# Last column transposes in another PSUM bank, six turn buffers, an earlier first tile of half two, and another order around the passage to layer 1

## The reference

```python
h = maximum(layernorm(x), 0)
# layer 0
S = relu((adj + adj.T) * 0.5); D = sum(S, axis=1); d = where(D > 0, D ** -0.5, 0)
L = eye - d[:, None] * S * d[None, :]
x = x + relu(L @ (h @ W0))
# layer 1
h = maximum(layernorm(x), 0)
x = x + diag(adj) @ (h @ W1[0]) + triu(adj, 1) @ (h @ W1[1]) + tril(adj, -1) @ (h @ W1[2]) + bias
```

## Time and profile before

| | |
|---|---|
| median of 3 runs | 958.63 us (954.3, 958.63, 959.94) |
| profiled execution, its own time | 957.01 us |
| its span in the profile | 955.2 us |
| PE busy | 909.1 us (95%) |
| DVE, ACT, POOL busy | 554.8, 492.6, 292.5 us |
| share of PE in the chain that ended last | 88% |
| mean granted TensorE clock | 0.992 |

### The profile page before, as it was taken

One profiled execution on the slowest core, in us unless ns is written; L12 is line 12 of the kernel. 1 busy time (PEld: TensorE's weight loads), 2 busy tenths in 40 slices (PEclk: granted clock), 3 DMA queues, 4 the chain that ended last, 5 costly groups with the idle time before them and its releaser, 6 DMA issues.

```text
span 955.2 us, 17248 instructions
## 1 busy us (share of the span) xinstructions
PE 909.1 (95%) x4471; PEld 767.5 (80%) x4471; DVE 554.8 (58%) x1461; ACT 492.6 (52%) x1042; POOL 292.5 (31%) x300
## 2 busy tenths in 40 slices
PE   3578999999999999999999998999999999999998
PEld 2467788888888888888888887888888888888886
DVE  3896777777878875656565655443433343334432
ACT  2898557666676665455545554343333333333331
POOL 4785344344434444434443441111111100000000
PEclk9999999999999999999999999999999999999999
DMA  9995799999999985565556556666666655555552
GB/s 285 312 273 149 251 317 333 321 352 322 349 323 339 340 286 207 176 198 161 158 177 196 165 163 192 199 202 189 192 183 185 192 167 164 167 164 159 162 169 68
DMA packets 179577, 212.68 MB, mean 223 GB/s; under 512 B 13648, under 2 KB 114000, under 8 KB 177488
## 3 DMA queue, kind: packets, MB, share of 16 engines
q1 hardware_dynamic: 136816, 158.18, 54.8%
q10 hardware_dynamic: 42720, 54.01, 16.2%
HBM read 143.99 MB, written 68.16 MB: 222 GB/s over the span
## 4 chain that ended last, share of the span: by engine, by line
PE 88%; DVE 3%; ACT 3%; DMA 2%; SPq 2%; issue 1%; ACTq 0%; DVEq 0%
PE psAcc L570 23%; PE psAcc L568 23%; PE psAcc L569 23%; PE psA L436 3%; PE psG L539 2%; PE psG L541 2%; PE psG L540 2%; PE psZ L501 2%; PE psW L408 1%; DMA colb<-in_adj 1%; ACT hst L600 1%; PE psG L408 1%; SPq L248 1%; PE psAcc L582 1%; PE psAcc L581 1%
## 5 line engine op out<-in xcount | busy, mean ns | idle before, releaser
L636 ACT ACTIVATE Lh<-C 128x512 fp32r<-128x512 f32 x256 | 161.5, 631 | 291.7 <-PE psAcc L570 249.4
L568 PE MATMUL psAcc<-Xh,Lh 128*128 128x512 f32 x496 | 199.7, 403 | 1.8 <-issue 1.4
L568 PE MATMUL psAcc<-Yh,Lh 128*128 128x512 f32 x512 | 200.9, 392 | 0.0
L570 PE MATMUL psAcc<-Yh,Ll 128*128 128x512 f32 x512 | 200.1, 391 | 0.0
L569 PE MATMUL psAcc<-Yl,Lh 128*128 128x512 f32 x512 | 199.9, 390 | 0.0
L570 PE MATMUL psAcc<-Xh,Ll 128*128 128x512 f32 x496 | 194.4, 392 | 0.0
L569 PE MATMUL psAcc<-Xl,Lh 128*128 128x512 f32 x496 | 194.0, 391 | 0.0
L823 DVE TENSOR_TENSOR Ll<-C,Lh 128x512 fp32r<-128x512 f32 x128 | 91.0, 713 | 142.9 <-ACT Lh L636 142.8
L570 PEld LDWEIGHTS psAcc<-Yh,Ll 128*128 128x128 f32 x512 | 96.1, 188 | 20.1
L569 PEld LDWEIGHTS psAcc<-Yl,Lh 128*128 128x128 f32 x512 | 96.2, 188 | 18.9
L568 PEld LDWEIGHTS psAcc<-Yh,Lh 128*128 128x128 f32 x512 | 96.2, 188 | 18.7
(11 more groups left out here) (130 smaller groups left out, 1356.5 us busy)
## 6 DMA issues: line engine op xcount, KB each, us to landing
C<-at_dram SPq DMA_DIRECT2D x128, 256.0 KB, 2.7
at_dram<-AT SPq DMA_DIRECT2D x16, 1088.0 KB, 5.4
s_dram<-C ACTq DMA_DIRECT2D x64, 256.0 KB, 5.4
R<-in_adj SPq DMA_DIRECT2D x64, 256.0 KB, 6.1
g_dram<-g ACTq DMA_DIRECT2D x32, 512.0 KB, 4.2
C<-s_dram SPq DMA_DIRECT2D x64, 256.0 KB, 3.9
C<-in_adj SPq DMA_DIRECT2D x60, 256.0 KB, 5.5
t_dram<-x ACTq DMA_DIRECT2D x32, 256.0 KB, 2.6
```

Source lines behind the costliest of these rows:

```text
L568: mm(acc, lh, rh[:, k, :], start=k == 0, stop=False)
L570: mm(acc, ll, rh[:, k, :], start=False, stop=c < L1 and k == NB - 1).then_inc(used, 1)
L636: A(Lh[:, q, :], C[:, q, :], ACT.Relu if s.c < L1 else ACT.Copy).then_inc(lhi, 1)
```

## The change

- The last group's column transposes go to `psW`, as all others do, and no longer wait for the turned tiles. `product0(12)` goes to `psAcc[:, 1]`, and `times_W0(13)`, which overwrites `psW`, waits for the reduction of all 7 groups.
- The turned tiles have six buffers instead of four (`x1[:, 1]` and `xe` are added).
- The prologue is written by tables only, slots -1 to 55. Within a slot ACT scales and splits before it normalises and turns; DVE does the degrees and rests before the statistics.
- The first xp: statistics on DVE in slot 39, ahead of the last `degrees`; the power on POOL behind the last `root`; normalised on ACT ahead of `scaled_hi(12)`; transposed ahead of the last two `rows_T` of step 0. In step 1 POOL's power for the second xp stands ahead of the masks, and ACT normalises it before it splits a quarter; its product with W0 stands after block 3 and not 7.
- Passage: SP loads the first `lx` and `g2` earlier in step 31; in steps 32 and 33 `slot` stands ahead of the last two `gev_out` and `t_out`; the first `result` is moved from the start of step 33 to its end on DVE.

```diff
-        SCALE_AT = [12, 13, 19, 20, 25, 26, 31, 32, 35, 36, 39]
+        COLS_AT = [9, 16, 22, 28, 32, 36, 40]
+        DEG_AT = [9, 17, 23, 29, 33, 37, 40]
+        ROOT_AT = [8, 16, 22, 28, 32, 36, 40]
+        TIMES_AT = [11, 12, 18, 19, 24, 25, 30, 31, 34, 35, 39, 40, 42, 42, 43, 43]
+        HIGH_AT = [12, 13, 19, 20, 25, 26, 31, 32, 35, 36, 39, 40, 44, 44, 44, 44]
+        LOW_AT = [14, 15, 21, 22, 27, 28, 33, 34, 37, 38, 40, 41, 44, 44, 44, 44]
+        MAIN_AT = [18, 19, 24, 25, 33, 34, 37, 38, 42, 42, 44, 44, 47, 47, 47, 47]
+        ROWS_AT = [41, 41, 46, 46]
+        COPY_AT = [42, 42]
+        XP_STAT, XP_POWER, XP_MEAN, XP_NORMAL, XP_TURN, SUM_AT = 39, 40, 42, 43, 45, 43
-        T0 = [z[:, :], h2[:, :], g12[:, 0, :], g12[:, 1, :]]
+        T0 = [z[:, :], h2[:, :], g12[:, 0, :], g12[:, 1, :], x1[:, 1, :], xe[:, :]]
-            return psZ[:, :] if j == 12 else psW[:, :] if j == 13 else psG[:, j % 2, :]
+            return psAcc[:, 1, :] if j == 12 else psW[:, :] if j == 13 else psG[:, j % 2, :]
@@ SP, body @@
+                    if q == 1 and c == L1 - 1:
+                        load_lx(nxt)
+                        load_g2(nxt)
-                if c == L1 - 1:
-                    load_lx(nxt)
-                    load_g2(nxt)
@@ PE, columns0 @@
-                dst = psW if e < len(GROUPS) - 1 else psAcc[:, 1, :]
-                if e == len(GROUPS) - 1:
-                    pe.wait_ge(t0_ok, NB)
@@ PE, times_W0 @@
                 if j == 13:
-                    pe.wait_ge(d_cols, len(GROUPS) - 1)
+                    pe.wait_ge(d_cols, len(GROUPS))
@@ ACT, turned0 @@
-                wait(act, w0_ok, j - 3)
+                wait(act, w0_ok, j - NT + 1)
@@ ACT, body @@
+                if L1 <= c < L1 + 2:
+                    slot(t)
                 if 2 <= c < L1 + 2:
                     gev_out(t, 2)
                     gev_out(t, 3)
-                if c >= L1:
+                if c >= L1 + 2:
                     slot(t)
@@ DVE, prologue @@
+                if XP_STAT == n:
+                    dve.wait_ge(ld_xp, 16)
+                    stats(npn, xp, p_st, p_mv, p_ve, 1)
+                if XP_MEAN == n:
+                    dve.wait_ge(p_rs, 1)
+                    neg_mean(npn, p_nm)
@@ DVE, body @@
-                if c > L1:
+                if c > L1 and c != L1 + 1:
                     result(t)
...
+                if L1 <= c < L1 + 2:
+                    slot(t)
                 if 2 <= c < L1 + 2:
                     t_out(t, 2)
                     t_out(t, 3)
                     wait(dve, tev, t.of(4, -4))
+                if c == L1 + 1:
+                    result(t)
                 if c < LAST - 1:
                     split_lo(nxt, 2)
-                if c >= L1:
+                if c >= L1 + 2:
                     slot(t)
```

More of the change, by code:

```diff
@@ L452, in _, with chunk_T @@
             pe.wait_ge(ld_w, 32)
-            for n, (k, g) in enumerate(CH0):
+            def chunk_T(n):
+                k, g = CH0[n]
                 i = NB - 1 - k
@@ L467, in _, with turn @@
                 last.then_inc(p0T, 1)
-                for e in range(len(COLS_AT)):
+            def turn(src, sem):
+                for b in range(HB):
+                    last = nc.tensor.transpose(psZ[:, b * F:(b + 1) * F], src[:, b * F:(b + 1) * F], ident[:, :])
+                last.then_inc(sem, 1)
+            for n in SLOTS:
+                if 0 <= n < len(CH0):
+                    chunk_T(n)
+                for e in range(len(GROUPS)):
                     if COLS_AT[e] == n:
@@ L473, in _ @@
                         turn0(j)
-                for j in range(len(SCALE_AT)):
-                    if SCALE_AT[j] - 1 == n:
+                for j in range(NB):
+                    if TIMES_AT[j] == n:
                         times_W0(j)
-                for j in range(len(MAIN_AT)):
+                for j in range(NB):
                     if MAIN_AT[j] == n:
                         main0(j)
[L480 to L502, removed]
+                for q in range(NQ):
+                    if ROWS_AT[q] == n:
+                        pe.wait_ge(p0S, len(CH0) - (1 if q % 2 == 0 else 0))
+                        rows_T(Step(None, 1), q)
+                if XP_TURN == n:
+                    pe.wait_ge(p_h, 1)
+                    pe.wait_ge(t0_ok, NB)
+                    turn(xp, yT)
             def finish(t, k):
                 c = t.c
-                if k == (7 if c == 1 else 3) and 1 <= c <= NB:
+                if k == 3 and 1 <= c <= NB:
                     if c == 1:
@@ L547, in body @@
                 if c == 1:
[L548 removed]
+                    pe.wait_ge(prep_lo, 13)
                 elif c < L1 + 2:
@@ L606, in turned0 @@
                 act.wait_ge(t0, j + 1)
-                wait(act, w0_ok, j - 3)
-                A(T0[j % 4], turned(j), ACT.Copy).then_inc(t0_ok, 1)
+                wait(act, w0_ok, j - NT + 1)
+                A(T0[j % NT], turned(j), ACT.Copy).then_inc(t0_ok, 1)
             def scaled_hi(j):
@@ L672, in turned_xp @@
                 A(yTs[:, :], psZ[:, :], ACT.Copy).then_inc(yT_ok, 1)
[L674 to L679, removed]
+            for n in SLOTS:
+                if 0 <= n < len(CH0):
+                    rectify(n)
+                for j in range(NB):
+                    if HIGH_AT[j] == n:
+                        scaled_hi(j)
+                for q in range(NQ):
+                    if SPLIT_HI_AT[q] == n:
+                        split_hi(Step(None, 0), q)
+                for j in range(NB + 1):
+                    if j < NB and NORMAL_AT[j] == n:
+                        normal0(j)
+                    if j and TURNED_AT[j - 1] == n:
+                        turned0(j - 1)
+                for q in range(2):
+                    if COPY_AT[q] == n:
+                        copy_T(Step(None, 1), q)
+                if XP_NORMAL == n:
+                    normal_xp(Step(None, 0))
             split_hi(Step(None, 1), 0)
-            normal_xp(Step(None, 0))
+            turned_xp(Step(None, 0))
             split_hi(Step(None, 1), 1)
             copy_T(Step(None, 1), 2)
-            turned_xp(Step(None, 0))
             split_hi(Step(None, 1), 2)
@@ L853, in degrees @@
                 w = min(hi, NB - 1) - lo
-                src = psW if e < len(GROUPS) - 1 else psAcc[:, 1, :]
                 dve.wait_ge(p0D, e + 1)
-                V.reduce_sum(drow[:, lo:lo + w, NQ], src[:, 0:w * P].rearrange("p (j c) -> p j c", c=P),
+                V.reduce_sum(drow[:, lo:lo + w, NQ], psW[:, 0:w * P].rearrange("p (j c) -> p j c", c=P),
                              axis=AX.X).then_inc(d_cols, 1)
@@ L883, in _ @@
                                 rowb[:, (NB - 1 - k) % 3, 4 * g * P:4 * g * P + w], ALU.add).then_inc(p0S, 1)
[L884 to L890, removed]
+            for n in SLOTS:
+                if 0 <= n < len(CH0):
+                    chunk_sum(n)
+                for e in range(len(GROUPS)):
                     if DEG_AT[e] == n:
                         degrees(e)
-                for j in range(len(SCALE_AT)):
-                    if SCALE_AT[j] + 2 == n:
+                for u in range(NB // 2):
+                    if MEAN_AT[u] == n:
+                        mean0(u)
+                for j in range(NB):
+                    if LOW_AT[j] == n:
                         scaled_lo(j)
-                for q in range(NQ - 1):
-                    if SPLIT_AT[q] + 2 == n:
+                for q in range(NQ):
+                    if SPLIT_LO_AT[q] == n:
                         split_lo(Step(None, 0), q)
[L899 to L911, removed]
+                if SUM_AT == n:
+                    sum_T(Step(None, 1), 0)
+                if XP_STAT == n:
[4 more added lines that the diff above has]
+                    neg_mean(npn, p_nm)
+                for j in range(NB):
+                    if STAT_AT[j] == n:
+                        stats0(j)
             split_lo(Step(None, 1), 0)
```

90 lines of the change are left out of this document (47 added, 43 removed).

## The result

The changed kernel takes **964.53 us** (median of 11 runs, 961.03 to 967.29); the kernel before took 958.63 in the same comparison (11 runs, 954.3 to 959.94). The ratio is 1.006, 95% interval 1.0045 to 1.0075: slower by 5.9 us, within 1% of no change. The profiled execution of the changed kernel took 967.29 us, span 965.4, the slowest of its 11.

A forecast was written before the change was run, and what follows sets the result against it. The prediction took PE to bound the steps. Its terms, -3.9 + 5.4 + 1.7 - 3.9 + 2.5 + 1.7 = +3.5 us, gave 960.5 on the profiled 957.01 or 962.1 on the median; it said 961 us, range 953 to 967.

The forecast's parts named there:

- two new waits: PE waits at the prologue's end (+5.4 us) and in step 34 (+2.5 us), each with +1.7 us of low clock.
- two gains: Second xp in step 1, -3.9 us, and the passage of steps 32 to 34, -3.9 us.
- First xp on DVE, +5.4 and +1.7: Prologue end: DVE waits for xp's load before the last degrees, holding PE's `times_W0(13)` 5.4 us; low clock adds 1.7.
- Column transposes, buffers, slot order, 0: Prologue: the 0.84 us wait before column transposes goes, but under the new wait; 0, or 0.8 without that wait.
- Second xp, -3.9: Step 1: an earlier load removes PE's wait before the second xp turn, 2.27 us, and the low clock, 1.66 us.
- `lx` -1.8, slots -1.5 and -0.6: Passage, steps 32 to 34: earlier `lx` load and slot copies remove PE's waits; together -3.9 us.
- `result` and the store, +2.5 and +1.7: Steps 33 and 34: the store waiting for late `result` delays SP's loads; PE waits 2.5 us, low clock adds 1.7.
- rival C: Both holds longer: later xp, work behind the reduction not fitting, or burst at 284 GB/s; 963 to 967 us, chance 0.16.
- rival A: Passage clean: burst at 408 GB/s or above, or loads overtake, so `t_dram` is in time; 956 to 958 us, chance 0.23.
- The clock behind a wait in a dense stretch: Step 34: a short wait may leave PE's clock alone, making the sum 1.7 us lower.
- The base: Whole kernel: +3.5 us on the profiled 957.01 gives 960.5; on the median 958.63 it gives 962.1; 961 was said.

The follow-up runs named there:

- the repeat: The changed kernel, unaltered, run once more for one profile: 965.52 us.
- Experiment 1: Changed kernel with SP issuing the first xp load ahead of the last strip's load: 958.56 us, ratio 0.9993 to the kernel before.
- experiment 11: Changed kernel with first xp load ahead of the last strip, step 33's store behind its loads, and four turn buffers instead of six: 954.08 us.
- experiment 5: Changed kernel with first xp load ahead of the last strip's load and step 33's store behind that step's loads: 954.06 us, ratio 0.9956 to the kernel before.
- experiment 10: Kernel before with only the changed passage and step 33's store behind that step's loads; prologue, steps 1 and 2 untouched: 955.53 us, ratio 0.9957.
- experiment 8: Changed kernel with the loads of lx and g2 for step 32 back at the end of SP's step 31: 966.65 us.
- experiment 9: Changed kernel with the two slot copies of steps 32 and 33 back behind the last evictions on ACT and DVE: 964.85 us.
- experiment 4: Changed kernel with SP issuing the store of step 33 behind that step's loads instead of ahead: 959.25 us, ratio 1.0006 to the kernel before.
- experiment 7: Changed kernel with first xp load and step 33's store moved, ACT's step 1 xp load issued earlier, early normalising extended to step 2: 955.43 us.

## Why the prediction was right, and where it was not

The forecast was 961 us in 953 to 967, by two new waits that outweigh two gains. 964.5 lies in the range, 3.5 above the forecast. That it is not further off is in part luck, since errors cancel: the first hold was forecast 1.1 us too high, the hold of step 34 by the medians 1.1 too low, and the gain on the second xp 2.4 too high. By its steps:

- **First xp on DVE, +5.4 and +1.7.** The mechanism was right, the size a little high. PE's `times_W0(13)` started 7.23 us later than in the trace before, 4.5 more than its prologue was; in the repeat 5.9 later, 5.1 more. From there to step 1 it lost 1.6 us to the low clock in both. Experiment 1 took 6.0 away, against the 7.1 of the forecast.
- **Column transposes, buffers, slot order, 0.** Right for the whole. The 0.8 us that I kept for a prologue without hold did not show: from the last chunk on ACT to `times_W0(13)` experiment 1 takes 4.7 us and the kernel before 4.8. In the trace of experiment 1 PE waits 1.60 us for ACT's z there, a wait that the trace before doesn't have at that place; that this took the place of the 0.84 us is my reading. The six buffers are worth 0 by experiment 11.
- **Second xp, -3.9.** The two parts were there, -3.8 in both traces of the changed kernel. What failed is that the prediction let PE keep all of it and put nothing against it in step 2. PE, no longer at 0.50, reached the turn of step 2 ahead of the chain on ACT and DVE and gave back 1.7 us in the repeat and 3.2 in the first trace (2.6 of it the wait, the rest stands under no wait). In the trace before that chain had its time from the low clock: experiment 5 enters step 2 2.78 us ahead of it, but ACT begins to normalise the xp of step 2 only 0.27 us ahead (127.76 against 128.03). The step fails as "the wait costs 2.27 and the low clock 1.66": removed, they are worth about 1.5, by experiment 5 against 10. This is the largest missed term, 2.4 us.
- **`lx` -1.8, slots -1.5 and -0.6.** Right: -3.7 by alignment, in both traces of the changed kernel and in experiments 5 and 10; of it the loads are 2.1 by the medians of experiment 8 and 1.8 by its alignment, and the slots 1.9 by the alignment of experiment 9.
- **`result` and the store, +2.5 and +1.7.** The mechanism was right, the size not: 5.9 us by the alignment, 5.3 by experiment 4, against 4.2. The burst did go out at 284 GB/s, the lowest of my three rates, and took 10.4 us; I had chosen between 284 and 334. That is rival C's rate and makes the forecast wait 3.5 us in place of 2.5. The rest lies in a row that I read wrongly. I took 0.68 us for the split of quarter 3 of step 34, the length of most splits, but this one took 1.62 us in the trace before already, and 1.59 in the changed kernel:
```profile
610.52 1.62 DVE L823 TENSOR_TENSOR Ll<-C,Lh 128x512 fp32r<-128x512 f32 x1
```
  With it the forecast wait would have been 4.4 us. Why it is longer than the others is open. The wait was 4.02 + 0.16 = 4.2 us and the low clock behind it 1.7. In the repeat the wait was 4.1 and the low clock cost 2.6; there the granted clock was 0.50 from 617 us on, 1.6 us before PE resumed. By the Trainium skill, page DMA: Bandwidth & Descriptors, section Where 436 GB/s comes from, the ceiling of the ports is 435 GB/s, and at that rate the burst would have given rival A. The same section puts the HBM side at about 358 GB/s for transfers between HBM and SBUF, by which the 2.95 MB would take an estimated 8.2 us. The burst of this trace stayed under both, at 284, while the window of 411 GB/s in the last section stands above the second.
- **The clock behind a wait in a dense stretch.** The Trainium skill, page TensorE: Matmul & The Clock Gate, section What's actually happening, was read as possibly leaving the clock alone in step 34. It fell: 0.59 over the 4.2 us behind the wait.
- **The base.** The trace of before (957.01) stood 1.6 under its median and had a favourable prologue. I put the sum on both bases and chose 961, nearer to the lower one; on the median the forecast would have been 962.

Sum as measured in the repeat, on its own 957.01: prologue +0.85, hold +5.1, clock +1.6, step 1 -3.8, steps 2 to 31 +1.8, passage -3.7, step 34 with its low clock +6.7, together 8.5, which is 965.52 - 957.01. The medians lie closer, 5.9 apart, since the trace of before was a favourable run and this one was not.

## What to carry to other kernels

An operation moved ahead takes its wait along: ask what the load it needs stands behind in its queue, and move the load first. Moving one load ahead in its queue took 6.0 us off, and moving one store behind its step's loads took off 5.3. When a wait and the low clock behind it are taken away, look which chain had used that time: here 1.7 to 3.2 of 3.8 us came back within three steps.

## What the runs showed of the hardware

Whether the clock falls behind a wait is not told by the length of the wait alone. PE was at 0.50 behind waits of 2.11 us (kernel before) and 2.17 us (experiment 10) at the turn of step 1. Behind 3.02 us in step 2 of experiment 7 the clock was 0.62 over the next 3 us. But it stayed at 1.00 behind the wait of 2.48 us in step 2 of the changed kernel:
```profile
138.30:140.30 2.00, 1.94 (x15) 1.91 (x15) 1.48 (x5) 1.12 (x3) 0.00 (x0) 1.00 1.05 411
```
In all four PE had been busy without a gap, at a clock of 1.00, for the 4 us before it went idle. What set them apart is open.

The issue of the bias took 4.69 us in the kernel before and 4.70 us in the changed one, and 3.6 to 4.7 us over all fourteen profiles. It was 3.6 to 4.4 in the five in which the load of xp no longer stood behind it, and 3.9 to 4.7 in the others, so the place of that load does not explain its length. What stands behind it in SP's queue is issued that much later.
